# A macaron transformer layer on eight cores: layer 1 of the coupling network from three half-size products, and the token tiles' residual split between ScalarE and VectorE

## The reference, cut to what matters

```python
def ffn(x):                                   # called twice, with the same weights
    gf = global_net(x.mean(axis=1))           # one number per sequence
    out = x
    for _ in range(3):                        # three cycles
        h = gelu(out @ w1 + b1)               # 1024 -> 1024
        h = gelu(h @ w2 + b2)                 # 1024 -> 512
        h = gelu(h @ w3 + b3)                 # 512 -> 256
        tf = sigmoid(h @ w4 + b4)             # 256 -> 1
        c = 0.1 + range * (0.7 * gf + 0.3 * tf - 0.5) * 2
        o_r, o_i, p_r, p_i = split(out, 4)
        out = out + c * concat([p_r, -p_i, -o_r, o_i])    # "twist"
    return out
x = x + 0.5 * ffn(layernorm(x))
x = x + attention(layernorm(x))               # causal linear attention and a memory
x = x + 0.5 * ffn(layernorm(x))
```

## Time and profile before

| | us |
|---|---|
| median of 3 runs (1989.95 to 1993.36) | 1992.2 |
| profiled execution, whole time | 1992.47 |
| its span, first to last instruction of core 0 | 1990.9 |
| spans of the other cores | 1983.4 to 1990.7 |
| TensorE busy | 1770.9 (89%) |
| VectorE busy | 1043.8 (52%) |
| ScalarE busy | 831.9 (42%) |
| GpSimd busy | 258.3 (13%) |

### The profile page before, as it was taken

One profiled execution on the slowest core, in us unless ns is written; L12 is line 12 of the kernel. 1 busy time (PEld: TensorE's weight loads), 2 busy tenths in 40 slices (PEclk: granted clock), 3 DMA queues, 4 the chain that ended last, 5 costly groups with the idle time before them and its releaser, 6 DMA issues.

```text
span 1990.9 us, 27826 instructions; the slowest of 8 cores (1983.4 to 1990.9 us)
## 1 busy us (share of the span) xinstructions
PE 1770.9 (89%) x8686; PEld 832.8 (42%) x8854; DVE 1043.8 (52%) x2138; ACT 831.9 (42%) x1242; POOL 258.3 (13%) x764
## 2 busy tenths in 40 slices
PE   0586889989988888999999999999998899999983
PEld 0343334434433344444444444444444344444431
DVE  5354355455456466555555555555542466656565
ACT  1454554554554551505050505050504455555552
POOL 2432201201211220000000000000100011111111
PEclk9788899999999998999999999999999999999997
DMA  8675321341272333111111111111322022222223
GB/s 187 149 210 136 49 86 64 94 132 72 91 170 89 138 120 114 64 64 64 64 64 64 64 64 64 64 64 64 83 72 85 12 85 85 96 96 84 76 85 127
DMA packets 50974, 181.93 MB, mean 91 GB/s; under 512 B 5776, under 2 KB 10384, under 8 KB 45200
## 3 DMA queue, kind: packets, MB, share of 16 engines
q0 software_dynamic: 29088, 89.93, 14.8%
q1 hardware_dynamic: 21744, 90.21, 14.2%
HBM read 123.23 MB, written 73.40 MB: 99 GB/s over the span
## 4 chain that ended last, share of the span: by engine, by line
PE 70%; DVE 11%; issue 8%; ACT 6%; POOL 2%; DMA 2%; DVEq 0%; SPq 0%; another core or an unknown queue 0%; ACTq 0%; POOLq 0%
PE ps L373 18%; PE ps L385 14%; PE ps L468 10%; PE ps L514 5%; PE ps L527 5%; PE ps L396 5%; PE ps L457 3%; PE ps L443 2%; DVE bnq L901 2%; ACT s_bf L811 2%; PE ps L344 2%; PE ps L531 2%; PE ps L489 2%; DVE xr L1025 1%; ACT xtok L651 1%
## 5 line engine op out<-in xcount | busy, mean ns | idle before, releaser
L373 PE MATMUL ps<-xt,w 128*128 128x512 bf16 x1501 | 373.5, 383 | 2.2 <-issue 0.4
L373 PEld LDWEIGHTS ps<-xt,w 128*128 128x128 bf16 x1536 | 152.1, 99 | 185.9 <-issue 9.9
L385 PE MATMUL ps<-h_c,w 128*128 128x512 bf16 x754 | 175.9, 390 | 18.2 <-ACT h_c L698 17.5
L385 PE MATMUL ps<-h_a,w 128*128 128x512 bf16 x748 | 176.2, 393 | 17.5 <-ACT h_a L698 16.1
L651 ACT ACTIVATE xtok<-xr,st_nmr,st_r 128x1024 bf16<-128x1024 f32 x32 | 37.1, 1230 | 289.4 <-POOL st_nmr L1253 289.4
L344 PE MATMUL ps<-idb,xtok 128*128 128x128 bf16 x768 | 64.8, 247 | 80.6 <-ACT xtok L651 77.7
L798 ACT ACTIVATE ebuf<-ps 128x512 bf16<-128x512 f32 x128 | 76.3, 597 | 137.0 <-PE ps L468 134.0
L1324 POOL DMA_DIRECT2D x_d<-xr x64 | 34.9, 546 | 756.9 <-DVE xr L1132 513.0
L1062 DVE TENSOR_SCALAR ebuf<-ebuf 128x512 bf16<-128x512 bf16 x128 | 37.8, 295 | 170.9 <-ACT ebuf L798 170.8
L514 PE MATMUL ps<-wmo,sq 128*128 128x512 bf16 x503 | 120.3, 383 | 4.8 <-DVE skt L1090 3.3
L385 PEld LDWEIGHTS ps<-h_c,w 128*128 128x128 bf16 x768 | 76.4, 100 | 113.4 <-issue 30.4
(11 more groups left out here) (202 smaller groups left out, 2748.8 us busy)
## 6 DMA issues: line engine op xcount, KB each, us to landing
x_d<-xr POOLq DMA_DIRECT2D x64, 512.0 KB, 2.9
xr<-x_d SPq DMA_DIRECT2D x64, 512.0 KB, 4.5
xt<-xn_d SPq DMA_DIRECT2D x22, 1024.0 KB, 6.3
x_ring<-hs SPq DMA_DIRECT2D x32, 512.0 KB, 6.8
xr<-hs SPq DMA_DIRECT2D x32, 512.0 KB, 9.2
xn_d<-stage POOLq DMA_DIRECT2D x16, 1024.0 KB, 4.3
out<-xr POOLq DMA_DIRECT2D x32, 512.0 KB, 3.2
xn_d<-spill POOLq DMA_DIRECT2D x6, 1024.0 KB, 5.7
```

The source lines that it names most:

```text
L373: i = te.matmul(out=ps[:, bk, :], lhsT=lhs, rhs=xt[:, slot, dt, :], start=(dt == 0), stop=(dt == DT - 1))
L385: i = te.matmul(out=ps[:, bks[et], :], lhsT=w2[:, kt, et * 128:(et + 1) * 128], rhs=ffn[ph]["h1"][:, kt, :], start=(kt == 0), stop=(kt == ...
```

## The change

With W1 in four row blocks, U and V share products: K = W_or (o_r + p_r) + W_pi (o_i + p_i), U = K + (W_pr - W_or) p_r + (W_oi - W_pi) o_i, V = K - (W_or + W_pr) o_r - (W_oi + W_pi) p_i. Each is a group of 4 matmuls in place of 8, so a block has 24 groups of 4, in the order K, U, V for each of eight output tiles. VectorE sums the features (`feature_sums`, `xs`) and prepares the weights (`prepare_w1`). ScalarE evicts K to `kt` (two buffers); VectorE evicts both U and V, adding `kt`. FILL places the 24 groups.

The four quarter operations of `combine` go to ScalarE (`spread`, buffers `tq`), one tile after the tanh of cycles 0 and 1, one ahead of `gelu2` in cycles 1 and 2. In A, tiles are normalized one at a time, and transposed in cycle 0 of the block after next. `tq_a` lies on the same memory as `stage2`, from which `xn_d` is stored. In B the statistics follow each tile, and the last block of A is combined and transposed later.

```diff
-FILL = [(2, 1, 3), (2, 1, 3), (2, 2, 0)]
...
+K_TILES = (0, 1, 6, 7)
+U_TILES = (2, 3, 4, 5)
+V_TILES = (0, 1, 6, 7)
...
+FILL = [(2, 2, 5), (2, 2, 5), (3, 3, 0)]
...
+            kt=sb("kt_" + ph, [128, 2, T], F32, r0 + 32768)[0],
+            xs=sb("xs_" + ph, [128, 4, T], BF16, r0 + 36864)[0],
...
+    tq_a, _ = sb("tq_a", [128, 2, D], F32, r0 + 8192)
...
     stage2, _ = sb("stage2", [128, DT, T], BF16, r0 + 8192)
+    stage2x, _ = sb("stage2x", [128, 2, DT, T], BF16, sf + 16384)
...
         def uv_group(ph, b, g):
-            et, is_v = uv_part(ph, b, g)
+            et, part = g // 3, g % 3
...
-                    te.wait_ge(*w1_ld.at("w1"))
...
             bk = take(("UV", ph, b, g))
-            for dt in range(DT):
-                if not is_v:
-                    lhs = w1[:, dt, et * 128:(et + 1) * 128]
+            for n in range(4):
+                if part == 0:
+                    lhs, rhs = w1[:, K_TILES[n], cols], ffn[ph]["xs"][:, n, :]
+                elif part == 1:
+                    lhs, rhs = w1[:, U_TILES[n], cols], xt[:, slot, U_TILES[n], :]
                 else:
-                    wt, neg = TWIST[dt]
-                    lhs = (ffn[ph]["w1n"][:, wt - 2, et * 128:(et + 1) * 128] if neg
-                           else w1[:, wt, et * 128:(et + 1) * 128])
-                i = te.matmul(out=ps[:, bk, :], lhsT=lhs, rhs=xt[:, slot, dt, :],
-                              start=(dt == 0), stop=(dt == DT - 1))
+                    lhs, rhs = ffn[ph]["w1n"][:, n, cols], xt[:, slot, V_TILES[n], :]
+                i = te.matmul(out=ps[:, bk, :], lhsT=lhs, rhs=rhs, start=(n == 0), stop=(n == 3))
             i.then_inc(bank_full[bk], 1)
...
             layer2(ph, b, k)
+            if ph == "A" and b > 1 and k == 0:
+                transposes("A", b - 2)
...
+        def k_group(ph, b, g):
+            et = g // 3
+            if g % 3 != 0:
                 return
             bk, use = banks.at(("UV", ph, b, g))
+            if et >= 2:
+                s.wait_ge(*freed_at(("UV", ph, b, g - 4)))
+            elif b > 0:
+                s.wait_ge(*freed_at(("UV", ph, b - 1, NG + g - 4)))
...
-                         bias=pack[:, P_B1 + et:P_B1 + et + 1]).then_inc(bank_free[bk], 1)
+            s.activation(out=ffn[ph]["kt"][:, et % 2, :], in_=ps[:, bk, :],
+                         func=AF.Copy).then_inc(bank_free[bk], 1)
+        def spread(ph, b, tt):
+            x, t, sc = xr[:, tt, :], spread_buffer(ph, b, tt), tk[:, b % 2]
+            s.wait_ge(*tok_ok.at((ph, b)))
+            s.wait_ge(*xr_ld[tt].at(xr_item(ph, 4 * b + tt)))
+            if ph == "A" and b < NB - 1:
+                if tt < 2 and b > 0:
+                    s.wait_ge(*xn_st.at((ph, b - 1)))
+                elif tt >= 2:
+                    s.wait_ge(*x_ok.at((ph, 4 * b + tt - 2)))
+            elif ph == "C" and b > 0:
+                s.wait_ge(*x_ok.at((ph, 4 * b + tt - 4)))
+            for q, src, m, a in ((0, 2, 1, 3), (1, 3, 2, 4), (2, 0, 2, 4), (3, 1, 1, 3)):
+                i = s.activation(out=t[:, q * 256:(q + 1) * 256],
+                                 in_=x[:, src * 256:(src + 1) * 256], func=AF.Identity,
+                                 scale=sc[:, m, tt:tt + 1], bias=sc[:, a, tt:tt + 1])
+            i.then_inc(*tq_ok.up((ph, b, tt)))
...
                 filler(ph, b, k - 1, 2)
-            if ph == "A" and b > 0 and k > 0:
-                normalize("A", b - 1, 2 * k - 2)
-                normalize("A", b - 1, 2 * k - 1)
+            if b > 0 and k == 1:
+                spread(ph, b - 1, 1)
+                if ph == "A":
+                    normalize("A", b - 1, 0)
+            if b > 0 and k == 2:
+                spread(ph, b - 1, 3)
+                if ph == "A":
+                    normalize("A", b - 1, 1)
+            if ph == "A" and b > 1 and k == 0:
+                normalize("A", b - 2, 3)
             gelu2(ph, b, k)
+            if ph == "A" and b > 1 and k == 0:
+                transposed("A", b - 2)
             filler(ph, b, k, 0)
...
                 gnet("C", 3)
+            if b > 0 and k < 2:
+                spread(ph, b - 1, 2 * k)
...
+        def uv_group(ph, b, g):
+            et, part = g // 3, g % 3
+            if part == 0:
                 return
+            k_done = freed_at(("UV", ph, b, 3 * et))
             bk, use = banks.at(("UV", ph, b, g))
+            v.wait_ge(*k_done)
             v.wait_ge(bank_full[bk], use + 1)
-            v.tensor_copy(out=ffn[ph]["v"][:, b % 2, et, :],
-                          in_=ps[:, bk, :]).then_inc(bank_free[bk], 1)
-        def negate_w1(ph):
+            if part == 1:
+                v.scalar_tensor_tensor(out=ffn[ph]["u"][:, b % 2, et, :], in0=ps[:, bk, :],
+                                       scalar=pack[:, P_B1 + et:P_B1 + et + 1],
+                                       in1=ffn[ph]["kt"][:, et % 2, :], op0=ALU.add,
+                                       op1=ALU.add).then_inc(bank_free[bk], 1)
+            else:
+                v.tensor_tensor(out=ffn[ph]["v"][:, b % 2, et, :], in0=ps[:, bk, :],
+                                in1=ffn[ph]["kt"][:, et % 2, :],
+                                op=ALU.add).then_inc(bank_free[bk], 1)
+        def feature_sums(ph, b):
...
+            x, xs = xt[:, b % 2], ffn[ph]["xs"]
+            v.tensor_tensor(out=xs[:, 0:2, :], in0=x[:, 0:2, :], in1=x[:, 4:6, :], op=ALU.add)
+            v.tensor_tensor(out=xs[:, 2:4, :], in0=x[:, 6:8, :], in1=x[:, 2:4, :],
+                            op=ALU.add).then_inc(*xs_ok.up((ph, b)))
...
+        def prepare_w1(ph):
...
+            w1n = ffn[ph]["w1n"]
...
+                v.wait_ge(*freed_at(("QK", "q", NB - 1, DT - 1)))
+            f = -1.0 if ph == "A" else -2.0
+            v.scalar_tensor_tensor(out=w1n[:, 0:2, :], in0=w1[:, 0:2, :], scalar=f,
+                                   in1=w1[:, 4:6, :], op0=ALU.mult, op1=ALU.subtract)
+            i = v.scalar_tensor_tensor(out=w1n[:, 2:4, :], in0=w1[:, 6:8, :], scalar=f,
+                                       in1=w1[:, 2:4, :], op0=ALU.mult, op1=ALU.subtract)
+            if ph == "A":
+                step(i)
+                v.tensor_tensor(out=w1[:, 4:6, :], in0=w1[:, 4:6, :], in1=w1[:, 0:2, :],
+                                op=ALU.subtract)
+                i = v.tensor_tensor(out=w1[:, 2:4, :], in0=w1[:, 2:4, :], in1=w1[:, 6:8, :],
+                                    op=ALU.subtract)
             i.then_inc(*w1n_ok.up(ph))
...
+            x = xr[:, tt, :]
+            v.wait_ge(*tq_ok.at((ph, b, tt)))
+            v.scalar_tensor_tensor(out=x, in0=x, scalar=tk[:, b % 2, 0, tt:tt + 1],
+                                   in1=spread_buffer(ph, b, tt), op0=ALU.mult,
+                                   op1=ALU.add).then_inc(*x_ok.up((ph, 4 * b + tt)))
...
         def cycle(ph, b, k):
             if k == 0 and b > 0:
                 token_couplings(ph, b - 1)
             if k > 0:
                 coupled(ph, b, k)
+                if b > 0:
+                    combine(ph, b - 1, 2 * k - 2)
                 filler(ph, b, k - 1, 2)
                 if k == 1:
                     turn(ph, b)
                 if b > 0:
-                    combine(ph, b - 1, 2 * k - 2)
                     combine(ph, b - 1, 2 * k - 1)
+            if ph == "A" and b > 1 and k == 0:
+                transposed("A", b - 2)
             filler(ph, b, k, 0)
             filler(ph, b, k, 1)
+            if k == 2 and b + 2 < NB:
+                feature_sums(ph, b + 2)
...
+            if b == 0:
+                for tt in range(NTT):
+                    combine("A", NB - 1, tt)
...
                     v.scalar_tensor_tensor(out=x, in0=ps[:, bk, :], scalar=rlm[:, 0, 0, tt:tt + 1],
                                            in1=x, op0=ALU.mult, op1=ALU.add).then_inc(bank_free[bk], 1)
-            statistics("B", b)
+                statistics("B", b, tt)
```

More of the change, by code:

```diff
@@ L617, in tensor_program @@
                     local_out(b, tt, eh)
+                if b == 0 and tt == 1:
+                    transposes("A", NB - 1)
             if b < NB - 1:
@@ L620, in tensor_program @@
                     state_group(b, g)
-        for g in range(16):
+        for g in range(NG):
             uv_group("C", 0, g)
@@ L664, in transposed @@
                 if ph == "A":
-                    s.activation(out=pair(stage2, bk2),
+                    s.activation(out=pair(stage_a(b), bk2),
                                  in_=src.rearrange("p (a t) -> p a t", a=2),
@@ L869, in scalar_program @@
         nc.scalar.preload_act_table_set("gelu_and_others")
-        for g in range(16):
-            u_group("C", 0, g)
+        for g in range(NG):
+            k_group("C", 0, g)
         transposed("B", NB - 1)
@@ L877, in scalar_program @@
                 cycle("C", b, k)
+        for tt in range(NTT):
+            spread("C", NB - 1, tt)
     def vector_program(v):
@@ L1078, in attention @@
```

(32 more changed lines are left out.)

184 lines of the change are left out of this document (86 added, 98 removed).

## The result

| | before | after |
|---|---|---|
| median, us | 1991.62 (4 runs, 1989.95 to 1993.36) | 2034.24 (4 runs, 2032.65 to 2107.21) |
| ratio, 95% interval | | 1.0211 (1.0191 to 1.0231) |
| span of core 0 | 1990.9 | 2033.3 |
| P, up to the first tanh of A | 174.5 | 165.6 (-8.9; forecast -9) |
| A, first tanh to last | 539.6 | 577.5 (+37.9; forecast +50) |

The 2107.21 us are of an execution in which the cores of one die had a lower granted clock (0.87 to 0.88 where the others had 0.92); the ratio leaves it out.

The account below looks back on a forecast made before the run. TensorE, holding 70% of the chain of waits, was taken as the bound. C +32, A +50, P -9, B -14 and -7, start of C -4 and end -4 make +44 on 1992.5: 2036 us, range 2003 to 2062.

Parts of the forecast that it names:

- The banks: Between cycles, `layer2`'s fourth bank waits for a U eviction behind `coupled` and a residual: start 9.2 us, idle 4.45.
- The clock: TensorE falls to half clock behind each new idle time: 1.7 us each, bounds 0 and 2.5.
- The rival with a clock that holds: None of the 23 new idle times lowers TensorE's clock: 39 us less, 1997 us, chance 0.09.
- The store: In A, `spread` ahead of cycle 1's gelus waits for `xn_d`'s store: idle 24.7 and 42.3 us in blocks 3 and 5.
- Blocks 2 and 4 of A: With 44 filler matmuls, only last gelus and one K eviction delay `layer2`, to 14.6: -0.5 us each.
- Block 6: In A: old stall and removed matmuls gain 14.5 us, store wait and second transition take 8.6 and 6.15: 0.
- Spread: Four quarter operations on ScalarE take 1.6 us; by the skill's figure 2.05, the sum some 4 us higher.
- P, B and the start of C: Gains outside the main stretches: P -9 us, B's block 0 -14, B's blocks 1 to 6 -7, start of C -4.
- the rival at 2063 us: VectorE's added evictions bind, so P and the start of B and C gain nothing: 2063 us, chance 0.18.
- The rivals at 1943 and 1967 us: Banks don't bind `layer2`: 1943 us, chance 0.04. The store doesn't hold ScalarE in A: 1967 us, chance 0.04.
- neither: Neither banks nor store bind: C 1 to 6 at -5.2 us each, A without stall, 1860 us, chance 0.02.

Follow-up runs that it names:

- two of the experiments: Against the changed kernel: first U eviction ahead of `coupled`, ratio to the kernel before 0.971; four filler groups in place 2, not five, 0.9726.
- the experiment: Changed kernel with B's statistics behind the last tile again: 2050.4 us in one execution, on a chip where the kernel before took 1995.4.
- with the bank free: Changed kernel with four filler groups in place 2, not five: ratio to the kernel before 0.9726, 1937 us on the changed kernel's scale.
- 0.9319: Changed kernel with store ahead of loads, four fillers in place 2, A's spreads, residuals and first normalization moved later: ratio 0.9319 to the kernel before.

## Why the prediction was right, and where its sizes were off

**The banks.** Right in mechanism and size: start at 9.27 (9.2), idle 4.36 (4.45). The U eviction took 0.74 where I took 0.69 from another line.

**The clock.** The mechanism was right; the term of 1.7 us for each idle time was too small by 0.6. Behind 4.29 us and more, the twelve `layer2` of C's blocks 1 to 6 took 8.75 to 9.70 us, 9.36 on average, 2.3 above 7.07. That is 7 of the 12 us missing in C. The rest is at its ends: block 0 lost 1.7 where I had 0, block 6 has fewer groups taken from it than a steady block and lost 8.3, block 7 lost 0.8. The rival with a clock that holds is refuted for this kernel; behind 1.15 to 1.35 us of idle, in two of the experiments, it does hold.

**The store.** Right: idle 25.8 and 40.1 us for 24.7 and 42.3, blocks 3 and 5 at +19.7 and +33.4 for +18 and +35.6. Block 1 is at -2.7 for -2.2.

**Blocks 2 and 4 of A.** Here a step failed: "only the last gelus and one K eviction delay `layer2`, to 14.6". It started at 10.57:

```profile
294.85 0.59 PE L417 MATMUL ps<-h_A,w4r 128*128 128x512 bf16 x2
...
305.42 6.85 PE L397 MATMUL ps<-h_a,w 128*128 128x512 bf16 x31 [0.49 <-DVE v_a L996]
...
292.67 0.23 POOL L1407 TENSOR_SCALAR tk<-tk 128x4 f32<-128x4 f32 x1 [0.16 <-POOL tk L1326]
```

I let POOL's factors come at 3.0 in the count from `layer4`, as in a short block. The fold groups make cycle 0 longer, so the factors were there 2.0 us before `layer4` (292.9), ScalarE waited 1.28 us for the store and the gelus were done in time. Only 0.4 to 0.5 us of idle time, full clock: -6.3 and -6.4 and not -0.5 each. These 12 us made up for the 12 missing in C: that the total came out within 2 us is luck. Block 0, priced at nothing, gained 4.0, and no experiment says why. Block 6 was at +4.7 for 0: 1.2 from the idle time (8.13 for 6.9), 2.0 from the half clock behind it and behind 4.29, 2.7 us each, and the rest, as in C, since its stretch from tanh to tanh has fewer groups taken from it.

**Spread.** Four quarters on ScalarE took 2.07 us, not 1.6. The figure of the Trainium skill ("ScalarE: Activation LUTs", section "Rules for kernel authors"), by which I had worked out 2.05, was right, and the row of a whole tile that I went by was not a measure for four short ones.

**P, B and the start of C.** -8.9 for -9. Block 0 of B gained 12.1 (14), blocks 1 to 6 gained 11.1 (7; the experiment puts it on the statistics), the last lost 1.3, the way into C gained 6.9 (4). VectorE's evictions did not become a bound there: P gained what was forecast and block 0 of B nearly so, and the rival at 2063 us is refuted.

**The rivals at 1943 and 1967 us** were what one gets by taking either wait away, and each was then measured: 1937 with the bank free, 1986 with the store moved ahead of the loads alone, since the ordinary store wait stays. The 1860 us of "neither" was reached within the noise: 0.9319 of 1992 is 1856 (1832 to 1881), the medians alone make 1871.

## What to carry to other kernels

Count what a group holds, not only what it costs: with banks handed out in turn, the n-th group from now takes the bank of one whose eviction may stand far back in another engine's row, and more filler can make the next stage later. When work moves to an engine with free time, ask for each of its waits what stands behind it there: a wait for a store or a tile put ahead of the critical gelus costs its whole length, while behind the gelus it held up nobody here, once the normalization had been moved too. An idle time on TensorE costs more than its length: behind 4.3 us the clock took 2.3 more on average, behind 1.3 nothing.
